# A fused cross-attention and feed-forward kernel: transposes by DMA, tiles of 128 rows, single products in TensorE's order, loads on ScalarE's queue

## What is computed

```python
x = x + xattn(layernorm(x), ctx, mask)      # q and out projection: int8-like rounding of rows and weights
x = x + ffn(layernorm(x))                   # both matmuls: int8-like rounding
# xattn, per batch: 16 heads of 32
q = (round(xn/sx) @ round(wq/sq).T) * (sx*sq) + bq        # sx per row: max|.|/127
k = ctx @ wk.T + bk ;  v = ctx @ wv.T + bv                # full fp32
p = softmax(q k^T / sqrt(32) + mask) ;  o = p v
out = (round(o/so) @ round(wo/swo).T) * (so*swo) + bo
# ffn: 512 -> 2048 -> 512
h = gelu((round(y/sy) @ round(W1/s1).T) * (sy*s1) + B1)
out = (round(h/sh) @ round(W2/s2).T) * (sh*s2) + B2       # sy, sh per row; s1, s2 one number per weight
```

## Time and profile before

| | |
|---|---|
| time, three runs | 769.23, 771.27 (median), 773.83 us |
| span of the profiled execution (first to last instruction) | 767.9 us |
| mean granted TensorE clock | 0.967 of 2.4 GHz |
| busy: TensorE / VectorE / ScalarE / GpSimd | 669.3 / 559.8 / 445.3 / 293.5 us |
| TensorE's weight loads | 517.3 us |
| chain that ended last | TensorE 78%, ScalarE 8%, VectorE 6% |
| DMA | 45.4 MB, one queue of SyncE, 18.8% of its engines' time |

### The profile page before, as it was taken

One profiled execution on the slowest core, in us unless ns is written; L12 is line 12 of the kernel. 1 busy time (PEld: TensorE's weight loads), 2 busy tenths in 40 slices (PEclk: granted clock), 3 DMA queues, 4 the chain that ended last, 5 costly groups with the idle time before them and its releaser, 6 DMA issues.

```text
span 767.9 us, 15796 instructions
## 1 busy us (share of the span) xinstructions
PE 669.3 (87%) x5576; PEld 517.3 (67%) x5576; DVE 559.8 (73%) x1270; ACT 445.3 (58%) x1084; POOL 293.5 (38%) x538
## 2 busy tenths in 40 slices
PE   0366989999999999999999999999999999997744
PEld 0255767777786777777777777786777777774522
DVE  2788675777878696869687777878696868677554
ACT  2312555666666675757666666666675757565501
POOL 1135152524344353535352524344353535231211
PEclk9998898999999999999999999999999999998778
DMA  9526641020302011121111020202011120000000
GB/s 303 222 62 212 225 155 42 4 72 1 86 2 74 14 42 45 33 55 33 55 31 55 3 85 2 83 5 74 14 38 49 35 66 10 25 2 25 1 13 12
DMA packets 24684, 45.38 MB, mean 59 GB/s; under 512 B 2144, under 2 KB 12128, under 8 KB 23984
## 3 DMA queue, kind: packets, MB, share of 16 engines
q1 hardware_dynamic: 24608, 44.38, 18.8%
HBM read 40.70 MB, written 3.67 MB: 58 GB/s over the span
## 4 chain that ended last, share of the span: by engine, by line
PE 78%; ACT 8%; DVE 6%; issue 4%; DMA 2%; POOL 2%; SPq 0%; POOLq 0%; DVEq 0%
PE ps_ring L797 30%; PE ps_t L827 13%; PE ps_ring L879 8%; PE ps_ring L897 7%; PE ps_s L820 7%; PE ps_t L839 6%; ACT L498 3%; PE ps_ring L866 2%; ACT pT L506 2%; PE ps_ring L790 2%; DMA pT<-in_wvT 1%; ACT probs L498 1%; PE ps_ring L886 1%; PE ps_ring L849 1%; ACT k_sb L485 1%
## 5 line engine op out<-in xcount | busy, mean ns | idle before, releaser
L506 ACT ACTIVATE pT<-ps_t 125x336 f32<-125x336 f32 x256 | 115.2, 450 | 169.1 <-PE ps_t L827 163.5
L498 ACT ACTIVATE probs<-probs,neg_max 112x375 f32<-112x375 f32 x256 | 153.2, 601 | 14.7 <-DVE neg_max L634 14.5
L827 PEld LDWEIGHTS ps_t<-ident,probs 112*125 112x125 f32 x768 | 112.8, 192 | 72.1 <-issue 38.2
L827 PE MATMUL ps_t<-ident,probs 112*125 112x112 f32 x768 | 132.8, 282 | 26.4 <-ACT probs L498 15.8
L634 DVE CUSTOM_DVE_ANT_0 probs<-ps_s,mask_in 112x375 f32<-112x375 f32 x256 | 130.6, 544 | 28.5 <-PE ps_s L820 21.4
L422 POOL TENSOR_TENSOR ctx_lo<-ctx_in,ctx_hi 128x376 fp32r<-128x376 f32 x64 | 66.0, 1035 | 90.5 <-ACT ctx_hi L480 90.4
L797 PE MATMUL ps_ring<-ctx_hi,wk_hi 128*128 128x376 f32 x256 | 92.6, 362 | 0.0
L797 PE MATMUL ps_ring<-wv_hi,ctx_hi 128*125 128x512 f32 x192 | 82.2, 428 | 8.3 <-POOL ctx_lo L422 8.3
L797 PE MATMUL ps_ring<-ctx_lo,wk_hi 128*128 128x376 f32 x256 | 86.1, 336 | 0.0
L797 PE MATMUL ps_ring<-ctx_hi,wk_lo 128*128 128x376 f32 x256 | 86.1, 336 | 0.0
L797 PE MATMUL ps_ring<-wv_hi,ctx_lo 128*125 128x512 f32 x192 | 77.6, 404 | 0.0
(11 more groups left out here) (123 smaller groups left out, 1289.4 us busy)
## 6 DMA issues: line engine op xcount, KB each, us to landing
ctx_in<-in_ctxT SPq DMA_DIRECT2D x32, 375.0 KB, 3.6
h<-in_w2T SPq DMA_DIRECT2D x4, 1024.0 KB, 5.4
b_row<-in_w2T SPq DMA_DIRECT2D x4, 1024.0 KB, 5.3
x_in<-in_x SPq DMA_DIRECT2D x16, 224.0 KB, 2.6
xres<-in_x SPq DMA_DIRECT2D x16, 224.0 KB, 2.6
out<-y SPq DMA_DIRECT2D x16, 224.0 KB, 3.6
mask_in<-in_mask SPq DMA_DIRECT2D x16, 164.1 KB, 3.6
w_q<-in_w1T SPq DMA_DIRECT2D x2, 1024.0 KB, 14.8
```

Of the source, the lines that this page charges most:

```text
L498: nc.scalar.activation(probs[:, hd % SP_RING, :], probs[:, hd % SP_RING, :], ACT.Exp, scale=-1.0, bias=neg_max[:, b % 2, hd:hd + 1], accum ...
L506: nc.scalar.activation(pT[0:LR, hd % PT_RING, :], ps_t[0:LR, 0:LC * N], ACT.Copy).then_inc(pT_s, 1)
L827: last = nc.tensor.transpose(ps_t[0:LR, lc * N:(lc + 1) * N], probs[:, hd % SP_RING, lc * LR:(lc + 1) * LR], ident[0:N, 0:N])
```

## The change

- Transposes of rounded rows (`x_T`, `o_T`, `y_T`, `h_T`) and of the rounded `wq` and `wo` become DMA transposes, SBUF to SBUF, issued by SyncE. The PSUM copies behind them are gone. The scales of x's rows go to DRAM and come back spread over 128 partitions (`xs_store`, `xs_load`); the scales of `wo` and of o's rows also pass through DRAM.
- Out projection and feed-forward work on 14 tiles of 128 consecutive rows instead of 16 of 112. `oqT` becomes a ring of 384 columns with margins, into which each batch's 112 columns are transposed (twice for the four batches that cross its end).
- One `k`, `v`, `T`, `out_proj`, `up` or `down` entry of TensorE's order is now one matmul (three for `k` and `v`). The five orders are strings of letters, one letter a unit, for the whole program.
- `T` and `PV` rotate through two banks of their own; the ring of the others has two banks instead of three.
- Context, x, mask, residual loads and the output's stores are issued by ScalarE, as letters of its order; SyncE keeps weights, transposes and scales.
- The preparation is cut into quarters that stand in the orders between the first context's work; `wq` is loaded first. The maximum over partitions becomes a TensorE transpose of a broadcast column and a VectorE reduce (`w_max`).
- Smaller ones: the norm's division by the standard deviation is folded into the scale of the rounding, so that the maximum of a row is taken beside the Newton steps; q's scale and bias work in place in `q_sb`; `v`'s three terms come in another order.

```diff
-SP_UNITS = (
-    ("down", 3, -3), ("prepare", 6, 1), ("mask_load", 0, 1), ...
-RING = 3
+TILES = B * N // P
+OQ, LEAD, TAIL = 3 * P, 96, 80
+RING = 2
+ATT = 2
+PE_UNITS = {
+    "M": ("w_max", each(2)),
+    "k": ("k", each(B, KC, KC)), "v": ("v", each(B, LC, KC)), "q": ("q", each(B)), "S": ("S", each(B, KC)),
+    "T": ("T", each(B, H, LC)), "P": ("PV", each(B, KC)), "g": ("gather", each(B)),
+    "o": ("out_proj", each(TILES, KC)), "u": ("up", each(TILES, 4, KC)), "d": ("down", each(TILES, FK)),
+}
+PE_ORDER = (
+    "kkkkkkkkkkkkkkkkvvvvvvvvvvvvkkkkkkkkqkkkkkkkkvSvvvTTTTTTSTTTvTTTvvPTMTTSTTTTTTvTTTPqTTTTTTSTTTvTTTvvPTTTvTTTTTTk"
...
+    "TTTTSkkkkkkkkkkkkqTTooooTTTTdSPTTTdvTTTTTTdvTTTdvTPTdTdvSTdTdTdTdTdTdTdTdTddTTTSPuTuTuTuuuTuTuTuuTuTuTuuuuvvvvPv"
...
+    "PTTdddddTTTdddTTTTTTuuPuuuuuuguuuuuuuuoooodddddddddddddddduuuuuuuuuuuuuuuudddddddddddddddd"
+DVE_ORDER = (
+    "babbabbaanbRbaaaabbbbwwwbnqRSSSSwSSSSwwwSSSSwwqSSSSwwnwwwgSoSSSwSSSSwRSSSSwSSSSwqwnSSSSwwgSoSSwwSwyRmSQwSwwSwSnS"
...
+    "qSSSSuSSSSduuuSShhSHSgoSSSSymSQSqSSuSSSSuuSuShhSSgoSSSSdHSSSSySmSQSSduuguuohhHymQduuuuhhHd"
+ACT_ORDER = (
+    "rccmxmWAAWAAWcWckkbxkWkWWWvAAvAAcvckkAAAkAkEEETTETvTEEEPETcTTcTvEPEETTETxETEmEPTETTvTAAAPAkkcEkEkTTEEcETTEEPTvET"
...
+SP_ORDER = (
+    "QWWWW1cQWWWW11tsXelft1slX2s2plo22X22slpoi22XYBslXHHpoislYXHHpoisYlXHHpsoilXYsHHpoisXYlpsoiHHYXlsHHpoiXlYspoXHlHp"
...
+def places(b):
+    at = LEAD + b * N % OQ
+    return [at] if at + N <= LEAD + OQ else [at, at - OQ]
...
+            def x_T(b):
+                sp.wait_ge(x_quant_s, b + 1)
+                wait_for(sp, q_pe, b)
+                sp.dma_start_transpose(xT[:, :, :], x_q[:]).then_inc(xT_in, 16)
+            def xs_store(b):
+                sp.wait_ge(x_scaled, b + 1)
+                wait_for(sp, xs_in, 16 * (b - 1))
+                sp.dma_start(xs_dram[b % 2].unsqueeze(1), x_s[:]).then_inc(xs_stored, 16)
+            def xs_load(b):
+                sp.wait_ge(xs_stored, 16 * (b + 1))
+                wait_for(sp, q_mul, b)
+                sp.dma_start(xs_bc[:], xs_dram[b % 2].partition_broadcast(P)).then_inc(xs_in, 16)
+            def o_T(b):
+                sp.wait_ge(o_quant_s, b + 1)
+                wait_for(sp, op_pe, -(-(N * (b + 1) - OQ) // P))
+                for at in places(b):
+                    sp.dma_start_transpose(oqT[:, :, at:at + N], o_q[:]).then_inc(oqT_in, 16)
+            def y_T(t):
+                sp.wait_ge(y_quant_s, t + 1)
+                wait_for(sp, up_pe, 4 * t)
+                sp.dma_start_transpose(yqT[:, :, :], y_q[:]).then_inc(yqT_in, 16)
+            def h_T(t, i):
+                sp.wait_ge(h_quant_s[i], t + 1)
+                wait_for(sp, down_pe, t)
+                sp.dma_start_transpose(hT[:, 8 * i:8 * i + 8, :], h_q[:, i * F // 2:(i + 1) * F // 2]).then_inc(hT_in[i], 16)
...
+            def ctx_load(b, i):        # on ScalarE
+                wait_for(act, ctx_lo_s, KC * (b - 1) + 2 * i + 2)
+                wait_for(act, ctx_hi_s, KC * (b - 1) + 2 * i + 2)
+                act.dma_start(ctx_in[:, 2 * i:2 * i + 2, 0:L], ctxT[b, ...]).then_inc(ctx_in_s[i], 16)
+            def x_load(b):
+                wait_for(act, x_quant_s, b)
+                act.dma_start(x_in[:], x[b]).then_inc(x_in_s, 16)
...
+            def down(t, k):
+                if k == 0:
+                    pe.wait_ge(hT_in[0], 16 * (t + 1))
+                    ring_bank("down", t, 0)
+                if k == FK // 2:
+                    pe.wait_ge(hT_in[1], 16 * (t + 1))
+                last = nc.tensor.matmul(bank_of("down", t, 0)[:, :], hT[:, k, :], w2_q[:, k, :], start=(k == 0), stop=(k == FK - 1))
```

More of the change, by code:

```diff
@@ L64 @@
-PE_UNITS = (
[6 rows of a table removed]
-)
[L72 to L83, removed]
-RING = 3
-RING_USES = [use for use in turns(PE_UNITS)
-             if use[0] in ("x_T", "q", "k", "v", "gather", "o_T", "out_proj", "y_T", "up", "h_T") or use[0] == "down" and use[2] == 0]
+LINKS = 3 + 2 * NEWTON
@@ new lines, with each @@
+RING = 2
+ATT = 2
+def each(*counts):
+    out = [()]
+    for n in counts:
+        out = [(*at, i) for at in out for i in range(n)]
+    return out
+PE_UNITS = {
[4 more added lines that the diff above has]
+}
+DVE_UNITS = {
+    "a": ("w_lo", each(2, KC)), "b": ("wqo", each(2, 6)), "w": ("prepare", each(2, 14)),
+    "n": ("x_norm", each(B)), "R": ("x_recip", each(B)), "q": ("q", each(B)), "S": ("S", each(B, H)),
+    "g": ("gather", each(B)), "o": ("o_quant", each(B)), "y": ("y_res", each(TILES)), "m": ("y_norm", each(TILES)),
+    "Q": ("y_quant", each(TILES)), "u": ("up", each(TILES, 4)), "h": ("h_absmax", each(TILES, 2)),
+    "H": ("h_quant", each(TILES)), "d": ("down", each(TILES)),
+}
@@ L90, with run @@
+RING_USES = [use for use in turns(PE_ORDER, PE_UNITS)
+             if use[0] in ("q", "gather", "w_max") or use[0] in ("k", "v", "out_proj", "up", "down") and use[1][-1] == 0]
 RING_AT = {use: n for n, use in enumerate(RING_USES)}
-ATT_USES = [use for use in turns(PE_UNITS) if use[0] in ("T", "PV")]
+ATT_USES = [use for use in turns(PE_ORDER, PE_UNITS) if use[0] == "PV" or use[0] == "T" and use[1][-1] == 0]
 ATT_AT = {use: n for n, use in enumerate(ATT_USES)}
-def run(eng, units, order):
-    for name, b, i in turns(order):
-        units[name](b, i)
+def run(eng, units, order, table):
+    for name, place in turns(order, table):
+        units[name](*place)
@@ L100, in xattn_ffn_kernel, with wait_for, wait_ring, tiles_of @@
+def wait_for(eng, s, count):
+    if count > 0:
+        eng.wait_ge(s, count)
+def wait_ring(pe, s, count):
+    pe.wait_ge(s, count)
+def tiles_of(b):
+    return b * N // P
+def batches_of(t):
+    return -(-(t + 1) * P // N)
+def places(b):
+    at = LEAD + b * N % OQ
+    return [at] if at + N <= LEAD + OQ else [at, at - OQ]
+def places_upto(b):
+    return sum(len(places(i)) for i in range(b))
 def xattn_ffn_kernel(nc, x, ctxT, mask, wq, bq, wkT, bk, wvT, bv, wo, bo, w1T, b1, w2T, b2, q_dram, out):
@@ L726, in _ @@
-            dve.wait_ge(c_in, 16 * 5)
-            units = {"prepare": prepare, "x_norm": x_norm, "x_quant": x_quant, "x_T": x_T, "q": q, "S": S, "gather": gather,
-                     "o_quant": o_quant, "o_T": o_T, "out_proj": out_proj, "y_norm": y_norm, "y_quant": y_quant,
-                     "y_T": y_T, "up": up, "h_absmax": h_absmax, "h_quant": h_quant, "h_T": h_T, "down": down}
-            run(dve, units, DVE_UNITS)
+                    wait_for(dve, h_quant_s[0], t)
+                if j == 2:
+                    wait_for(dve, h_quant_s[1], t)
@@ L745, in _, with ring_bank @@
-            pe.wait_ge(so_diag, KC)
-            for m in range(KC):
-                last = nc.tensor.matmul(ps_ring[2][0:N, m * P:(m + 1) * P], ones[:, 0:N], w_diag[:, m, :], start=True, stop=True)
-            last.then_inc(so_bcast, 1)
-            pe.wait_ge(w_lo, 2)
-            pe.wait_ge(wqo_evac, 2 * KC)
-            pe.wait_ge(so_ready, 1)
-            def ring_bank(name, b, i):
-                n = RING_AT[name, b, i]
+            def ring_bank(name, *place):
+                n = RING_AT[name, place]
@@ L903, in _ @@
-            run(pe, units, PE_UNITS)
+            units = {"w_max": w_max_unit, "q": q, "k": k_unit, "v": v_unit, "S": S, "T": T, "PV": PV, "gather": gather, "out_proj": out_proj,
+                     "up": up, "down": down}
+            run(pe, units, PE_ORDER, PE_UNITS)
 _OUT = (B, N, C)
```

1048 lines of the change are left out of this document (506 added, 542 removed), and 12 rows, old and new, of tables (ACT_UNITS, PE_UNITS).

## The result

The changed kernel takes 768.1 us in the median of 16 runs (759.7 to 774.7), the kernel before 771.1 us in 16 (768.2 to 773.8): a ratio of 0.994, with a 95% interval of 0.991 to 0.996: 0.6% faster, where 12% was forecast (675 us).

What follows compares the result with a forecast made beforehand. TensorE was taken to bound the steady part, with waits and low clock at both ends. Slots of 583 plus losses of 24 (start), 28 (middle), 8 and 29 (end) gave 672 of span, so 675 us, range 640 to 735.

Steps and rivals of the forecast that it cites:

- the part on VectorE, GpSimd and ScalarE: Other engines: VectorE gains slack, GpSimd idles over half the period, ScalarE's 2.7 us of new issues a batch are covered.
- rival (b): SyncE's transposing queue becomes the bound: T of 7.4 us passes TensorE's 38; 831 us at T = 9.5; chance 0.07.
- the sum: Whole program: TensorE's slots 583 plus losses 24, 28, 8 and 29 give a span of 672 us.
- The transposes' landing, taken as 3 us: Transposing DMAs out of SBUF: each lands in 3 us, covered by the gaps before out projection and up.
- the prediction's estimate: From the skill page: 26 blocks fill 34 us of SyncE's queue, h transposes land after 10 us, sum near 710.
- Middle, 38.0 us a batch: Steady part: slots fall by 3.2 us a period to 38.0; loss there 28 us instead of 32.
- the slots: TensorE's work, start to start, over the whole program: falls from 638.6 to 583 us.
- Start: Until the first S: first k product at 13, first S at 45; 24 us lost instead of 55.
- End, 42.5 us behind the last gather: Last gather to program end: 42.5 us against 39.1, of which 13.5 slots and 29 lost (25 to 40).
- Rival (c): ScalarE's queue stalls: waiting loads hold up exponentials by 1 to 2 us a batch, say 700 us; chance 0.16.
- Rival (a): Landings uncovered: a transpose lands in 6 us instead of 3, delaying out projection and up by 44: 719 us; chance 0.12.
- (d): No gain: static lists drift against each other and eat 6 us a period, about 771 us; chance 0.05.

Runs made afterwards that it cites:

- run 13: The changed kernel with o's scale written 16 times over, so its store into DRAM is 112 rows of 64 bytes: 697.5 us.
- run 4: The changed kernel without the store and load of o's and x's scales, constants in their place: 665.4 us.
- run 11: The changed kernel with x's scales carried by TensorE and o's by two on-chip DMAs a tile, whole reference computed: 667.1 us.
- after: The changed kernel itself, against the kernel before: 768.1 us, ratio 0.994.
- run 6: run 4 plus one unread store a batch of 112 four-byte elements into DRAM, ahead of o's transpose: 737.1 us.
- run 10: run 4 plus one unread store a batch of 112 rows of 64 bytes into DRAM, ahead of o's transpose: 666.4 us.
- run 7: run 4 plus one unread store a batch of 112 rows of 512 bytes into DRAM, ahead of o's transpose: 671.1 us.
- run 8: run 4 plus one unread store a batch of 112 four-byte elements on chip, ahead of o's transpose: 667.5 us.
- run 2: The changed kernel with the two small stores of scales (x and o) issued by GpSimd instead of SyncE: 761.1 us.
- run 12: The kernel before with an unread store of 112 four-byte scales into DRAM once a batch on SyncE's queue: 837.8 us.

## Why the prediction was wrong

**The step that failed** is the last sentence of the part on VectorE, GpSimd and ScalarE: "SyncE's queue only carries what the transposes need, in list order: 4.9 transposes and 3.9 small DMAs a batch." The small DMAs are in rival (b) alone, with the time of their issue; in the sum they stand at nothing, and nowhere is there a term for their landing. They were the new round trips of the scales, a new kind of DMA in this kernel, and the prediction gave no reason why other work should hide them, as it did for the transposes. The landing of a store is 7.7 us, and the round trips cost 103 us (768.1 - 665.4).

Could the rows have told? The kernel before has no store of small elements. Its one row of small elements, bq_col with 10.4 us, is a load, and the prediction set it aside as belonging to the crowded first microseconds. That was right: of the loads around it one of 224 KB, issued 2.5 us later, took 9.7, and in run 13 four-byte elements are loaded in 2.2 us (cols<-q_dram above).

```profile
bo_row<-in_bo SPq DMA_DIRECT2D x1, 224.0 KB, 9.7
```

So no row had the price. What the prediction could have done is to name the term and say that nothing in the rows bounds it.

**A second step was missing**: that one DMA can hold up another. The sum took each landing by itself. The held transpose is what TensorE waited for: 64.7 us in the changed kernel, 7.4 in run 4, where nothing holds it.

The other steps, read in run 4, where the round trips are gone:
- *The transposes' landing, taken as 3 us*: right. 2.4 (o), 3.3 (h, eight blocks of 128x128), 2.3 (y), 3.0 (x); only those of the preparation, beside the weights' loads, land later (wq 8.1, wo 5.0). The issue of one takes 1.2 to 1.27 us of SyncE's queue in the median, far from the 7.4 at which rival (b) would begin. The figure of the Trainium skill, page VectorE: DVE Perf Modes, section The three transpose paths, 1309 ns for a 128x128 block, can't be multiplied as the prediction's estimate did: its 10 us for eight blocks are 3.3 here, 0.4 us a block, and the measurement decides. A single block was not measured.
- *Middle, 38.0 us a batch*: 36.4 in the mean. The prediction says that the slots fall to 38.0, but 38.0 is the old period less 3.2, with the old loss of 2.2 still in it; the slots alone are 583/16 = 36.4. Up to the last gather run 4 loses 51.9 us (621.4 less slots of 583 - 13.5), where the sum had 24 + 28 + 8 = 60. In run 11 TensorE is busy 41.00 of 41.00 us. VectorE, at 23 to 30 of 41 in the steady stretches of runs 4 and 11, was no bound.
- *Start*: the first k product at 13, measured 11.3; the first S at 45, measured 49.8 in run 4 and 55.3 in after, where q waited for x's scales. The first gather came 32 us earlier in after and 37 in run 4 (76.0), against the 31 of the forecast.
- *End, 42.5 us behind the last gather*: 42.4 in run 4 (621.4 to 663.8), 46.6 in after.
- *Rival (c)*, ScalarE's queue: TensorE's wait for the exponentials is 3.4 us over run 4. It didn't happen. *Rival (a)*, landings of 6 us for all transposes, has the right symptom in one place, o's, but it is no property of the transposes, and its price of 44 us is half of what was lost; *(d)* had nearly the measured time, 771, by a mechanism that run 4 refutes. The worth of the second bank for the transposes was not measured apart.

So the sum was right to 10 us (665 against 675) for a kernel without the round trips, and the miss of 93 us for the changed kernel is the term that it left out.

## What to carry to other kernels

A change that takes a value across partitions by way of DRAM has a price in its landing, not in its issue: find the width of its elements first, write rows of at least 64 bytes (the least that was tried and found quick), or move it on chip, where the same four-byte elements were harmless. Read a DMA's landing together with what was issued in the few us ahead of it, on any queue: if two end together, suspect the earlier one and leave it out in a run of its own; here reordering the two within the list only moved the wait. And when waits appear on TensorE, look at its busy time and granted clock behind them too: in run 6 a third of the cost was the lower clock.

## What the runs showed of the hardware that I had not expected

- A store of 112 four-byte elements from 112 partitions into DRAM lands in 6.4 to 9.0 us in the median. Rows of 64 bytes to the same memory land in 1.5 and 1.6 us (runs 10 and 13), rows of 512 in 1.6 (run 7), and four-byte elements on chip in 1.8 to 2.4 (runs 8 and 11). The Trainium skill, page DMA: Bandwidth & Descriptors, section Specifications, gives 512 bytes as the least for full rate, and says that below it the engine reads, modifies and writes; by these runs 64 bytes land as soon as 512, and if it is the width that counts, the step lies between 4 and 64. Widths between and four-byte elements spaced apart were not tried, nor what in the chip makes the four-byte write late.
- A DMA issued while such a store is in flight is not done before it, whichever queue either is in: the transpose of o lands in 7.2 us with the store in GpSimd's queue (run 2), the context's loads of ScalarE's queue in 7.5 (run 6), the output's store in 9.8 (run 12). In runs 6 and 12 all 61 DMAs issued while one was in flight landed at least 0.16 us behind it, and all 27 that were in flight when one was issued landed before it; in run 2, with two such stores a batch, at most two of 57 issued behind did not land behind. The same page, section Queues, rings and completion order, says that the write which signals a DMA's end lands only behind every earlier write of that DMA engine, across its queues. The trace agrees: in run 12 the small store, issued at 437.94, and the output's, at 438.44, both land between 448.1 and 448.3. That such an order is the whole cause of the hold is not shown: the context's loads of run 6 landed 1.2 to 6.7 us behind the store, not with it.
- A transposing DMA of four or eight blocks takes 1.2 to 1.27 us of the issuing queue, and lands 2.3 to 3.3 us behind its issue when no such store holds it (medians of run 4, the preparation's left out).
